# Cross-attention's keys and values projected in the first stage, y kept in SBUF

## The chip, the cores and the metric

The kernel runs on one core of a Trainium2 chip. The metric is the device time of one execution in microseconds, as the median of several runs. TensorE (PE in the profile) multiplies matrices, VectorE (DVE) and ScalarE (ACT) work elementwise, GpSimd (POOL) does a little beside them, and SyncE (SP) issues nearly all transfers. SBUF is the memory beside the engines, PSUM (`bank`, eight banks of 128 x 512 f32) takes TensorE's results, HBM holds inputs, output and scratch.

## The reference

One decoder layer over 8 batches of 512 tokens, width 512, in three sublayers, each with a norm. The first is a self-attention with 16 heads and fake quantisation: every tensor is divided by a power of two that comes from its own absolute maximum, rounded, and multiplied again. The second is a cross-attention to a context of 8 x 512 x 384, the third a feed-forward net. What matters here:

```python
h = layernorm(x) * fq_round(gamma) + fq_round(beta)
qkv = fq_floor(fq_floor(h) @ fq_round(w_qkv))
...
y = fq_floor(fq_floor(out) @ fq_round(w_out))
x1 = layernorm(x + y)
# cross-attention, 16 heads of 32
q = x1 @ Wq + bq
k = ctx_768 @ Wk + bk
v = ctx_768 @ Wv + bv
```

Keys and values of the cross-attention depend on the context alone; its queries depend on all of the self-attention.

## The kernel before

It is written by hand in stages. At the end of a stage every engine drains and calls `barrier(e, k)`, a semaphore that counts all five. The order of an engine's work is the order of the code; between engines semaphores alone set it (`wait_ge`, `then_inc`). SBUF is one `arena` that `Carve` divides anew for each stage, so a stage hands its results on through scratch in HBM. Batches run in loops of two (`batches`, `through`, `ahead`), with double buffers chosen by `par`.

**Start.** SP loads gamma, beta and the temperature (L409 to L411). VectorE takes the peaks of gamma and beta, GpSimd reduces them over the partitions (`over_partitions`), VectorE forms the powers of two (`power_of_two`) and the temperature's exponential. Then barrier 1, and only after it the first load of `x`.

**First norm** (`first_norm`, `turn_z`, `store_h`). For each batch VectorE takes statistics (`norm_stats`), writes the normed z (L1423), waits until TensorE has transposed its 16 tiles into PSUM (L788), applies gamma and beta from PSUM (L1437), and takes the peak of |h| (L1335 with `stats`). h goes to scratch, since its scale is known only after all batches. ScalarE issues the loads of `w_qkv` and `w_out` and computes nothing. After the last batch VectorE takes the peaks of the two weight matrices and quantises them (L1450 to L1453). Barrier 2; the next stage starts with the load of h (L437).

**Stages 3 to 7** size and compute the self-attention. Stage 7 leaves its result `oG` in SBUF.

**Stage 8**, the output projection (`project`, `y_out`, `quantise_o`, `peak_y`): TensorE projects, ScalarE copies PSUM into `yH`, VectorE takes the peak, SP stores `y` to scratch (`store_y`).

**Stage 9**, the cross-attention projections, per batch. SP loads context, x and y (L541 to L543). TensorE transposes the context (12 transposes, L931), computes V (12 matmuls, L938) and K (12, L943), transposes x1 (16, L950) and computes the queries (16, L957); each f32 matmul appears as two instructions in the trace. PSUM banks are claimed in turn. ScalarE evacuates every unit (`project_evac`: L1235 context, L1239 V, L1241 x1, L1245 K and queries with bias). VectorE quantises y, adds it to x and norms (L1634 on; `split_qk`), adds the value bias (L1642), and splits keys and queries into two f16 halves, which the next stage multiplies (L1647, L1648). SP stores x1, V and the halves; barrier 9 waits for them.

## Time and profile before

| what | value |
|---|---|
| median of 3 runs | 3355.82 us (3354.48 to 3357.97) |
| the profiled execution | 3351.47 us, its span 3349.7 us |
| TensorE busy | 2680.5 us, 80% of the span |
| VectorE busy | 2548.2 us, 76% |
| ScalarE busy | 1450.3 us, 43% |
| GpSimd busy | 158.8 us, 5% |
| moved between SBUF and HBM | 341 MB, mean 102 GB/s |
| mean granted clock of TensorE | 0.881 of full speed |

The span runs from the first to the last instruction on the chip. The shares are means over stages with different limits, so they say little of one stage. Times in the rows count from the span's start, and what ended an engine's idle time stands in brackets behind a row. DMA rows (SPq, ACTq) show the issue of transfers, not their duration. A granted clock of 1.00 is 2.4 GHz, 0.50 is 1.2 GHz.

### The profile page before, as it was taken

What the parts mean: (1) busy time and instruction counts of PE and PEld (TensorE: products, weight loads), DVE (VectorE), ACT (ScalarE), POOL (GpSimd) and SP (SyncE); (2) the same over time, 40 slices, a digit from 0 to 9 for tenths busy, and PEclk for the clock granted to TensorE, in tenths of its full rate; (3) what the DMA queues carried; (4) which work ended last, traced back from release to release, by engine and by line L of the source; (5) the groups of instructions that cost most, each with busy time, mean ns of one, the idle gap of its engine ahead of it and who ended that gap; (6) DMA issues with size and microseconds to landing.
All of it is one profiled execution on the core that took longest, in us unless ns stands there. A gap on an engine that the chain in (4) does not pass through costs nothing. (4 is left out here: it accounts for less than half of the span.)

```text
span 3349.7 us, 46340 instructions
## 1 busy us (share of the span) xinstructions
PE 2680.5 (80%) x13160; PEld 1043.6 (31%) x13160; DVE 2548.2 (76%) x4627; ACT 1450.3 (43%) x2397; POOL 158.8 (5%) x146
## 2 busy tenths in 40 slices
PE   1169899867777466667799979999999739999998
PEld 1124322211111233333344422222223324444443
DVE  5878599999999799998455559888886884544454
ACT  0000244359999899995222225555552002122111
POOL 0000233200000000000000000111110000000000
PEclk7579999955555799999899989999999959999999
DMA  5221122233333233332545543344445410100000
GB/s 201 100 82 63 63 88 108 99 104 126 120 123 113 98 109 94 104 97 73 191 169 175 175 119 90 102 111 111 108 152 204 180 42 1 49 27 26 25 26 26
DMA packets 198800, 341.15 MB, mean 102 GB/s; under 512 B 32536, under 2 KB 118552, under 8 KB 187280
## 3 DMA queue, kind: packets, MB, share of 16 engines
q1 hardware_dynamic: 194464, 322.90, 29.5%
q10 hardware_dynamic: 4208, 16.78, 1.3%
q8 instruction: 51, 0.84, 0.1%
q14 instruction: 77, 0.63, 0.1%
HBM read 200.70 MB, written 138.90 MB: 101 GB/s over the span
## 5 line engine op out<-in xcount | busy, mean ns | idle before, releaser
L1335 DVE TENSOR_REDUCE stats<-bank 128x1024 f32 (+1 forms) x352 | 408.0, 1217 | 66.3 <-PE bank L798 33.0
L1193 ACT ACTIVATE arena<-arena,scale 128x512 bf16<-128x512 int8 x512 | 408.1, 798 | 53.4 <-DVE arena L1530 53.4
L858 PE MATMUL bank<-arena 64*128 64x512 bf16 x512 | 306.1, 604 | 105.1 <-DVE arena L1523 66.8
L1211 ACT ACTIVATE arena<-arena,scale 128x512 f32<-128x512 int8 x512 | 367.1, 802 | 12.8 <-DMA arena<-dq_scr 12.8
L1523 DVE CUSTOM_DVE_ANT_0 arena<-bank,arena,fac 128x512 int8<-128x512 f32 x512 | 349.5, 746 | 23.5 <-PE bank L858 11.4
L1662 DVE TENSOR_REDUCE arena<-bank 128x2 f32<-128x1024 f32 x256 | 312.5, 1223 | 54.5 <-PE bank L968 38.7
L1279 ACT ACTIVATE arena<-bank 128x1024 f32<-128x1024 f32 x256 | 248.0, 1022 | 187.8 <-PE bank L984 187.8
L1313 ACT ACTIVATE arena<-bank,arena,fac 128x512 f32<-128x512 f32 x128 | 99.5, 777 | 456.8 <-PE bank L1136 456.8
L798 PE MATMUL bank<-arena 128*128 128x512 bf16 x1024 | 246.6, 385 | 60.9 <-DVE arena L1465 52.5
L1012 PE MATMUL bank<-arena 128*32 128x512 f32 x2048 | 270.1, 604 | 0.0
L875 PE MATMUL bank<-identb,arena 128*128 128x128 bf16 x2048 | 138.9, 222 | 148.7 <-DVE arena L1572 148.7
L1863 DVE TENSOR_SCALAR arena<-arena 128x512 f16<-128x512 f32 x128 | 54.7, 427 | 260.6 <-ACT arena L1313 260.6
L1144 PE MATMUL bank<-arena 128*128 128x512 f16 x1024 | 242.0, 379 | 1.7 <-DVE arena L1864 1.3
L1133 PE MATMUL bank<-arena 128*128 128x512 f16 x1024 | 241.9, 379 | 0.0
L1572 DVE TENSOR_SCALAR arena<-arena 128x512 bf16<-128x512 f32 x512 | 221.8, 480 | 24.8 <-ACT arena L1211 24.4
L875 PEld LDWEIGHTS bank<-identb,arena 128*128 128x128 bf16 x2048 | 116.7, 99 | 210.1 <-DVE arena L1572 166.6
L1181 ACT ACTIVATE arena<-bank,floor_c,fac 128x1024 int8<-128x1024 f32 x96 | 115.5, 1204 | 150.1 <-PE bank L798 95.6
L968 PE MATMUL bank<-arena 128*128 128x512 f16 x512 | 157.2, 391 | 22.3 <-DMA arena<-half_scr 13.4
L1688 DVE TENSOR_SCALAR arena<-arena 128x1024 f32<-128x1024 f32 (+1 forms) x192 | 165.9, 864 | 7.8 <-ACT arena L1279 7.8
L1181 ACT ACT_TABLE_LOAD x4 | 5.1, 1283 | 382.7 <-PE bank L798 382.7
L858 PEld LDWEIGHTS bank<-arena 64*128 64x128 bf16 x512 | 51.5, 101 | 359.8 <-DVE arena L1523 349.5
L1555 DVE TENSOR_SCALAR arena<-bank 128x2048 bf16<-128x2048 bf16 x128 | 155.7, 1216 | 0.0
(193 smaller groups left out, 3641.0 us busy)
## 6 DMA issues: line engine op xcount, KB each, us to landing
dq_scr<-arena SPq DMA_DIRECT2D x128, 256.0 KB, 2.0
arena<-dq_scr SPq DMA_DIRECT2D x128, 256.0 KB, 2.6
arena<-half_scr SPq DMA_DIRECT2D x256, 128.0 KB, 2.8
qkv_scr<-arena SPq DMA_DIRECT2D x8, 3072.0 KB, 9.6
arena<-in_x SPq DMA_DIRECT2D x16, 1024.0 KB, 7.1
arena<-qkv_scr SPq DMA_DIRECT2D x128, 128.0 KB, 2.3
x_scr<-arena SPq DMA_DIRECT2D x16, 1024.0 KB, 3.9
half_scr<-arena SPq DMA_DIRECT2D x32, 512.0 KB, 3.8
```

The costliest lines, as they stand in the source:

```text
L798: last = mm(dst, wqkv_q[:, k, P * u:P * u + P], hq[:, k, :], start=k == 0, stop=k == KC - 1)
L858: return mm(dst, qE[r, h // 2, P * t:P * t + P], kE[r, h // 2, :], start=True, stop=True)
L875: last = nc.tensor.transpose(PT[s % 2][:, j, P * t:P * t + P], aG[:, s % 2, t, P * j:P * j + P], identb[:, :])
L1012: last = mm(bank[XD * g:XD * g + XD, 7 if k < 2 else 6, :], w, eT[:, par, g, c, :], start=c == 0, stop=c == NT - 1)
L1133: mm(dst, Wf[:, k, P * s:P * s + P], xx[:, par, k, :], start=k == 0 and n == 0, stop=False)
L1144: mm(bank[:, t, :], gg[:, f % 3, P * t:P * t + P], Wp[:, f, :], start=f == 0 and n == 0, stop=False)
L1193: last = A(e_dump[:, NT * (h % 2) + t, :], dq8[:, h % 4, t, :], ACT.Exp, bias=negm_b[:, par, c:c + 1], scale=scale[:, S_DOTS:S_DOTS + 1], ...
L1211: A(eG[:, s % 2, t, :], dqG[:, s % 4, t, :], ACT.Exp, bias=negm_g[:, par, c:c + 1], scale=scale[:, S_DOTS:S_DOTS + 1]).then_inc(S("eG_done ...
L1279: A(eT[:, r % 2, 2 * a:2 * a + 2, c, :], bank[:, 2 + 2 * a:4 + 2 * a, :], ACT.Exp, scale=XSCALE / HALF ** 2).then_inc(S("eX_done"), 1)
L1335: return V.tensor_reduce(dst, src, ax, ALU.max, apply_absolute_value=True)
L1523: V.tensor_tensor_reduce(dq8[:, s, t, :], bank[:, 4 * (h % 2) + t, :], floor_row, fac[:, C_DOTS:C_DOTS + 1], -3.0e38, ALU.add, ALU.max, ac ...
L1662: V.tensor_reduce(mxX[:, mp, hs, 2 * u:2 * u + 2], bank[:, at:at + 2, :], AX.X, ALU.max).then_inc(S("sX_red"), 1)
```

## The change

Keys and values are projected in the first stage; barrier 1 is left out; `y` stays in SBUF; the later stage projects the queries alone.

- **SP** issues the loads of `x`, the context, `Wv`, `Wk`, the key bias (`bk16`) and the value bias (`bv_s`) at once behind gamma, beta and the temperature. In the first stage it also stores V and the key halves. Their completion is waited for at barrier 3. `Wq`, the query bias and the first two tiles of x for the residual are loaded during stage 8.
- **TensorE** in the first stage: context and V of batch 0, z's transposes of batch 0, K of batch 0; from then on z, context with V, and K of each batch. z takes banks 0 to 3, the rest takes banks 4 to 7 in turn (`kv_bank`). In stage 9 it transposes x1 one batch ahead of the queries.
- **ScalarE** applies gamma and beta (`h_out`, which was VectorE's L1437), and evacuates context, V and K in the first stage. In stage 8 it copies `y` into the part of `oG` that has been read (`y_of`).
- **VectorE** norms in place (`zB` is gone), one batch ahead. Gamma and beta are made ready after norm 0 (`gamma_beta`). The value bias and the key split come into the first stage. The peaks of the weights come in batch 2, their scales in batch 3, quantising in batches 3 to 5. In stage 9 the residual norm runs two batches ahead of the split of the queries.
- Loops over batches in these stages are written out.
- `y_scr` is gone; `first_norm`, its counters and the numbers of the partition reductions are renumbered to match.

The core of the diff (removed lines are left out where new code stands in their place):

```diff
-            barrier(sp, 1)
...
+            load_x(0)
+            load_ctx(0)
+            for dst, src in ((Wv_s, Wv), (Wk_s, Wk)):
+                sp.dma_start(dst, chunk(src)).then_inc(S("wI_in"), 16)
+            load_x(1)
+            with nc.allow_non_contiguous_dma(reason="a column of 512 numbers"):
+                sp.dma_start(bk16, col(bk)).then_inc(S("wI_in"), 16)
+            sp.dma_start(bv_s, bv.rearrange("(a n) -> a n", a=1).broadcast_to([P, D])).then_inc(S("wI_in"), 16)
+            load_ctx(1)
...
+            for b in range(NB):
+                if b + 2 < NB:
+                    sp.wait_ge(S("z_turned"), b * NT + NT)
+                    load_x(b + 2)
+                    sp.wait_ge(S("kv_mm"), b * UNITS_K + CC)
+                    load_ctx(b + 2)
+                sp.wait_ge(S("h_ready"), b * KC + KC)
+                sp.dma_start(h_scr[b], hB[:, b % 2]).then_inc(S(f"h_stored{b % 2}"), 16)
+                sp.wait_ge(S("v_ready"), b * NT + NT)
+                for o in range(KC):
+                    sp.dma_start(v_scr[b * KC + o], vI[:, :, P * o:P * o + P]).then_inc(S("v_stored"), 16)
+                sp.wait_ge(S("split_done"), b * KC + KC)
+                for n in (0, 1):
+                    sp.dma_start(half_scr[2 + n][b * KC:b * KC + KC].rearrange("o p t -> p o t"), k_halves[:, n]
+                                 ).then_inc(S("k_stored"), 16)
...
+            def load_x1(b):
+                if b >= 2:
+                    sp.wait_ge(S(f"x_in{b % 2}"), 8 * NB + 16 * (b // 2))
+                sp.dma_start(x1_of[b % 4], tok(x[b])).then_inc(S(f"x_in{b % 2}"), 16)
+            sp.dma_start(Wq_s, chunk(Wq)).then_inc(S("wI_in"), 16)
+            with nc.allow_non_contiguous_dma(reason="a column of 512 numbers"):
+                sp.dma_start(bq16, col(bq)).then_inc(S("wI_in"), 16)
+            for b in (0, 1):
+                load_x1(b)
...
+            for b in (2, 3):
+                load_x1(b)
+            for b in range(NB):
                 sp.wait_ge(S("x1_ready"), b + 1)
...
+                sp.dma_start(x1_scr[b], x1_of[b % 4]).then_inc(S("x1_stored"), 16)
+                sp.wait_ge(S("split_done"), (NB + b) * KC + KC)
+                for n in (0, 1):
+                    sp.dma_start(half_scr[n][b * KC:b * KC + KC].rearrange("o p t -> p o t"), q_halves[:, b % 2, n]
+                                 ).then_inc(S(f"q_stored{b % 2}"), 16)
+                if b + 4 < NB:
+                    sp.wait_ge(S("x1_turned"), b * KC + KC)
+                    sp.wait_ge(S("x1_stored"), 16 * b + 16)
+                    load_x1(b + 4)
...
+            pe.wait_ge(const_made, 7)
...
+            def kv_bank(b, n):
+                before = b * UNITS_K + n - 4 if n >= 4 else (b - 1) * UNITS_K + (UNITS_K - 3 + n if n < 3 else UNITS_K - 4)
+                if before >= 0:
+                    pe.wait_ge(S("kv_evac"), before + 1)
+                return bank[:, 4 + n % 4, :]
+            def ctx_values(b):
+                pe.wait_ge(S(f"c_in{b % 2}"), 16 * (b // 2) + 16)
+                for k in range(CC):
+                    dst = kv_bank(b, k)
+                    for t in range(NT):
+                        last = nc.tensor.transpose(dst[:, P * t:P * t + P], cx[:, b % 2, t, P * k:P * k + P], ident[:, :])
+                    last.then_inc(S("kv_mm"), 1)
+                for t in range(NT):
+                    dst = kv_bank(b, CC + t)
                     if t == 0:
...
+                        pe.wait_ge(S("kv_evac"), b * UNITS_K + CC)
+                    for k in range(CC):
+                        last = mm(dst, cxT[:, k, P * t:P * t + P], Wv_s[:, k, :], start=k == 0, stop=k == CC - 1)
+                    last.then_inc(S("kv_mm"), 1)
+            def ctx_keys(b):
+                for o in range(KC):
+                    dst = kv_bank(b, CC + NT + o)
+                    for k in range(CC):
+                        last = mm(dst, Wk_s[:, k, P * o:P * o + P], cxT[:, k, :], start=k == 0, stop=k == CC - 1)
+                    last.then_inc(S("kv_mm"), 1)
+            pe.wait_ge(S("wI_in"), 16 * 4)
+            ctx_values(0)
+            turn_z(0)
+            ctx_keys(0)
+            for b in range(1, NB):
+                turn_z(b)
+                ctx_values(b)
+                ctx_keys(b)
...
+            def queries(b):
+                pe.wait_ge(S("x1T_done"), b * KC + KC)
                 for o in range(KC):
...
+                    if b:
+                        pe.wait_ge(S("q_evac"), (b - 1) * KC + o + 1)
                     for k in range(KC):
...
+                        last = mm(bank[:, 4 + o, :], Wq_s[:, k, P * o:P * o + P], x1T[:, b % 2, k, :],
+                                  start=k == 0, stop=k == KC - 1)
+                    last.then_inc(S("q_mm"), 1)
+            turn_x1(0)
+            for b in range(NB):
+                if b + 1 < NB:
+                    turn_x1(b + 1)
+                queries(b)
...
+            def h_out(b):
+                act.wait_ge(S("z_turned"), b * NT + NT)
+                if b >= 2:
+                    act.wait_ge(S(f"h_stored{b % 2}"), 16 * (b // 2))
+                    act.wait_ge(S("h_peak"), b - 1)
+                for k in range(KC):
+                    A(hB[:, b % 2, k, :], bank[:, k, :], ACT.Identity, bias=bet[:, k:k + 1], scale=gam[:, k:k + 1]
+                      ).then_inc(S("h_ready"), 1)
+            def values_kept(b):
+                for n in range(CC + NT):
+                    act.wait_ge(S("kv_mm"), b * UNITS_K + n + 1)
+                    src = bank[:, 4 + n % 4, :]
+                    if n < CC:
+                        A(cxT[:, n, :], src, ACT.Copy).then_inc(S("kv_evac"), 1)
+                    else:
+                        if n == CC and b:
+                            act.wait_ge(S("v_stored"), 64 * b)
+                        A(vI[:, n - CC, :], src, ACT.Copy).then_inc(S("kv_evac"), 1)
+            def keys_kept(b):
+                for o in range(KC):
+                    n = CC + NT + o
+                    act.wait_ge(S("kv_mm"), b * UNITS_K + n + 1)
+                    if b:
+                        act.wait_ge(S("split_done"), (b - 1) * KC + o + 1)
+                    A(t32[:, o, :], bank[:, 4 + n % 4, :], ACT.Identity, bias=bk16[:, o:o + 1], scale=HALF
+                      ).then_inc(S("kv_evac"), 1)
+            values_kept(0)
+            act.wait_ge(S("gam_ready"), 1)
+            act.wait_ge(S("b16_ready"), 1)
+            h_out(0)
+            keys_kept(0)
+            for b in range(1, NB):
+                h_out(b)
+                values_kept(b)
+                keys_kept(b)
...
+            def x1_turned_out(b):
+                for k in range(KC):
+                    act.wait_ge(S("x1_turned"), b * KC + k + 1)
+                    if k == 0 and b >= 2:
+                        act.wait_ge(S("q_mm"), (b - 1) * KC)
+                    A(x1T[:, b % 2, k, :], bank[:, k, :], ACT.Copy).then_inc(S("x1T_done"), 1)
+            def queries_out(b):
+                for o in range(KC):
+                    act.wait_ge(S("q_mm"), b * KC + o + 1)
+                    if b:
+                        act.wait_ge(S("split_done"), (NB + b - 1) * KC + o + 1)
+                    A(q32[:, o, :], bank[:, 4 + o, :], ACT.Identity, bias=bq16[:, o:o + 1], scale=HALF
+                      ).then_inc(S("q_evac"), 1)
+            x1_turned_out(0)
+            for b in range(NB):
+                if b + 1 < NB:
+                    x1_turned_out(b + 1)
+                queries_out(b)
...
+            def h_peak(b):
+                dve.wait_ge(S("h_ready"), b * KC + KC)
+                amax(stats[:, b:b + 1], hB[:, b % 2], AX.XY).then_inc(S("h_peak"), 1)
...
+            first_norm(0)
+            gamma_beta()
+            for b in range(NB):
+                h_peak(b)
+                if b + 1 < NB:
+                    first_norm(b + 1)
+                bias_values(b)
+                if b == 2:
+                    weight_peaks()
+                if b == 3:
+                    weight_scales()
+                if b in (3, 4):
+                    quantise_wqkv(2 * b - 6)
+                    quantise_wqkv(2 * b - 5)
+                if b == 5:
+                    quantise_wout()
+                split_keys(b)
...
+            def residual_norm(b):
+                ch = Chain(dve, S("norm_step"), 2 + NORM, b, NB * NORM)
+                x1 = x1_of[b % 4]
+                dve.wait_ge(S(f"x_in{b % 2}"), 8 * NB + 16 * (b // 2) + 16)
+                ch.link(V.tensor_scalar(y8, y_of[b], fac[:, C_Y:C_Y + 1], FLOOR, ALU.mult, ALU.add))
+                ch.link(V.scalar_tensor_tensor(x1, y8, sc(S_Y), x1, ALU.mult, ALU.add))
+                norm_stats(ch, x1)
                 for t in range(NT):
...
+                    last = normed(x1[:, t, :], x1[:, t, :], t)
                 last.then_inc(S("x1_ready"), 1)
...
+            for b in (0, 1):
+                residual_norm(b)
+            for b in range(NB):
+                if b + 2 < NB:
+                    residual_norm(b + 2)
+                split_queries(b)
```

## Rows read from the trace of the kernel before

**Rows 1.** Windows of two stages; columns: us, busy time (instructions) by engine, PEclk, DMA share, GB/s.
```profile
23.00:149.00 126.00, 28.91 (x128) 26.06 (x128) 95.15 (x234) 0.00 (x0) 0.00 (x0) 0.61 0.53 196
1620.00:1964.00 344.00, 308.74 (x864) 147.61 (x864) 173.39 (x369) 90.73 (x152) 0.00 (x0) 0.96 0.50 173
```

**Rows 2.** Timeline of the first stage; columns: start, duration, engine, line, operation.
```profile
23.37 1.15 SPq L419 DMA_DIRECT2D arena<-in_x  x2
...
31.85 2.13 ACTq L1171 DMA_DIRECT2D arena<-in_L_attn_w_qkv  x4
...
43.91 2.46 DVE L1398 BATCH_NORM_STATS2 bn<-arena 128x6 f32<-128x512 f32 x4
...
53.70 2.96 DVE L1437 TENSOR_SCALAR arena<-bank,gam,bet 128x512 f32<-128x512 f32 x4 [2.47 <-PE bank L788]
...
56.78 2.29 DVE L1335 TENSOR_REDUCE stats<-arena 128x2048 f32 x1
...
58.98 2.46 DVE L1398 BATCH_NORM_STATS2 bn<-arena 128x6 f32<-128x512 f32 x4
```

**Rows 3.** Timeline of the weight work after the first norm.
```profile
149.59 17.41 DVE L1335 TENSOR_REDUCE peak<-arena 128x1 f32<-128x12288 f32 x2
...
169.27 1.82 DVE L1450 TENSOR_SCALAR arena<-arena,inv 128x3072 int8<-128x3072 f32 x1
...
188.83 1.06 SPq L437 DMA_DIRECT2D arena<-h_scr  x2
```

**Rows 4.** Timeline of one batch of the cross-attention projections.
```profile
1677.56 1.68 PE L931 MATMUL bank<-ident,arena 128*128 128x128 f32 x12
...
1690.58 2.49 DVE L1642 TENSOR_TENSOR arena<-arena 128x512 f32<-128x512 f32 x4
...
1700.74 1.91 PE L950 MATMUL bank<-ident,arena 128*128 128x128 f32 x16
...
1701.02 0.69 ACT L1245 ACTIVATE arena<-bank,arena 128x512 f32<-128x512 f32 x1 [1.89 <-PE bank L943]
...
1701.61 2.05 ACT L1241 ACTIVATE arena<-bank 128x512 f32<-128x512 f32 x4
...
1702.20 0.69 DVE L1648 TENSOR_TENSOR arena<-arena 128x512 f16<-128x512 f32 x1
...
1703.71 14.00 PE L957 MATMUL bank<-arena 128*128 128x512 f32 x32 [1.06 <-ACT arena L1241]
...
1717.55 1.68 PE L931 MATMUL bank<-ident,arena 128*128 128x128 f32 x12
```

**Rows 5.** Groups of instructions on the page: the GELU evacuation.
```profile
L1313 ACT ACTIVATE arena<-bank,arena,fac 128x512 f32<-128x512 f32 x128 | 99.5, 777 | 456.8 <-PE bank L1136 456.8
```

**Rows 6.** Timeline at both ends of the cross-attention stage.
```profile
1619.35 0.16 DVE L1624 TENSOR_TENSOR fac<-fac,inv 128x1 f32<-128x1 f32 x1
...
1620.82 0.40 SPq L529 DMA_DIRECT2D arena<-in_L_xattn_Wq  x1
...
1632.02 0.17 DVE L1629 TENSOR_SCALAR arena<-arena 128x8 f32<-128x8 f32 x1 [12.50 <-DMA arena<-in_L_xattn_bv]
...
1639.25 1.29 DVE L1634 TENSOR_SCALAR arena<-arena,fac 128x2048 int8<-128x2048 f32 x1 [7.07 <-DMA arena<-y_scr]
...
1650.20 2.49 DVE L1642 TENSOR_TENSOR arena<-arena 128x512 f32<-128x512 f32 x4
...
1958.97 0.69 DVE L1648 TENSOR_TENSOR arena<-arena 128x512 f16<-128x512 f32 x1
```

**Rows 7.** Windows around idle stretches of TensorE and its restart.
```profile
0.00:41.00 41.00, 3.48 (x16) 3.24 (x16) 15.34 (x64) 0.00 (x0) 1.88 (x12) 1.00 0.35 127
1614.00:1618.00 4.00, 0.00 (x0) 0.00 (x0) 2.92 (x5) 0.33 (x1) 0.36 (x1) 1.00 0.11 45
1958.00:1961.00 3.00, 0.00 (x0) 0.00 (x0) 1.12 (x2) 0.47 (x1) 0.00 (x0) 0.83 0.11 38
1634.00:1642.00 8.00, 7.18 (x17) 4.27 (x18) 2.71 (x2) 1.79 (x3) 0.00 (x0) 0.50 1.04 394
```

More of the change, by code:

```diff
@@ L40 @@
 DUOS = QKV_UNITS // 2
[L41 removed]
+UNITS_K = CC + NT + KC
 NEXT_AT = (7, 9, 11, 13)
@@ L905, in project @@
                 for t in range(NT):
-                    pe.wait_ge(S("y_evac"), b * NT + t + 1)
+                    if not (isinstance(b, int) and b < 2):
+                        pe.wait_ge(S("y_evac"), b * NT + t + 1 - 2 * NT)
                     for k in range(PAIRS):
@@ new lines, in split_keys @@
+            def split_keys(b):
+                ch = Chain(dve, S("split_step"), KC, b)
+                if b:
+                    dve.wait_ge(S("k_stored"), 32 * b)
+                for o in range(KC):
+                    dve.wait_ge(S("kv_evac"), b * UNITS_K + CC + NT + o + 1)
+                    ch.link(V.tensor_copy(k_halves[:, 0, o, :], t32[:, o, :]))
+                    V.tensor_tensor(k_halves[:, 1, o, :], t32[:, o, :], k_halves[:, 0, o, :], ALU.subtract
+                                    ).then_inc(S("split_done"), 1)
+                ch.end()
@@ new lines, in _ @@
+            first_norm(0)
+            gamma_beta()
+            for b in range(NB):
+                h_peak(b)
[12 more added lines that the diff above has]
+                split_keys(b)
@@ L1615, in quantise_o @@
                     peak_y(b - 1, 1 - par)
-            through(dve, quantise_o)
+            for b in range(NB):
+                quantise_o(b, b % 2)
             peak_y(NB - 1, 1)
-            dve.wait_ge(S("y_peak"), 2 + NB)
+            dve.wait_ge(S("y_peak"), NB)
             link(amax(peak[:, S_Y:S_Y + 1], stats[:, 0:NB]))
@@ L1650, in split_qk, with split_queries @@
-                ch.end()
-            batches(dve, split_qk)
+                ch.end()
+            def split_queries(b):
+                ch = Chain(dve, S("split_step"), KC, b, NB * KC)
+                if b >= 2:
+                    dve.wait_ge(S(f"q_stored{b % 2}"), 32 * (b // 2))
+                for o in range(KC):
+                    dve.wait_ge(S("q_evac"), b * KC + o + 1)
+                    ch.link(V.tensor_copy(q_halves[:, b % 2, 0, o, :], q32[:, o, :]))
+                    V.tensor_tensor(q_halves[:, b % 2, 1, o, :], q32[:, o, :], q_halves[:, b % 2, 0, o, :], ALU.subtract
+                                    ).then_inc(S("split_done"), 1)
+                ch.end()
@@ L1652, in _ @@
+            for b in (0, 1):
+                residual_norm(b)
+            for b in range(NB):
+                if b + 2 < NB:
+                    residual_norm(b + 2)
+                split_queries(b)
             barrier(dve, 9)
```

330 lines of the change are left out of this document (113 added, 217 removed).

## The prediction

> **What bounds the kernel now.** I began with windows cut at the barriers, which show how busy each engine is by stage, and went to timelines of one batch in the two stages that the change touches, to see which wait ends last. The others (369 to 1548 us, and from 1964) keep their instructions, and I give them no change.
>
> The windows show two opposite stages [rows 1]. From 23 to 149 us TensorE is busy 28.9 of 126 us, VectorE 95.2, and ScalarE not at all. From 1620 to 1964 TensorE is busy 309 of 344 us, VectorE half, ScalarE a quarter. In the first stage a batch takes 15.07 us, from one row of statistics (43.91) to the next (58.98), and the chain is VectorE's own: norm, wait for TensorE's transposes (2.47), gamma and beta (2.96), peak [rows 2]. After the eighth batch VectorE alone runs 39 us, the weight peaks of 17.4 us and the quantising; the next stage's first load goes out at 188.83 [rows 3]. In the cross-attention stage a batch takes 39.99 us (1677.56 to 1717.55), and TensorE waits in it about 2 us in all, 1.06 of it ahead of the queries [rows 4]. VectorE there waits for ScalarE, which waits for TensorE: the stage is TensorE's.
>
> So TensorE's work is carried from a stage that it fills to one where it has room. What it costs there depends on what the first stage becomes.
>
> **The first stage after.** Each batch gives TensorE 16 transposes of z (1.91 us, as 1700.74), 12 of the context (1.68, as 1677.56), and 24 instructions for V and 24 for K. The 32 for the queries take 13.84 us (1703.71 to 1717.55), 0.4325 each, so V and K take 20.8 [rows 4]. ScalarE evacuates in program order: four h tiles, then three context tiles, then V, then K; V cannot start before the third context tile is out. Counted from the end of z's transposes that is 0.28 us to ScalarE's start (K ends at 1700.74, the copy starts at 1701.02), four h tiles, three copies and 0.1 to hand over. Plain copies run at a pitch of 0.51 us (four in 2.05) [rows 4]. An evacuation with a per-partition scale and bias appears only as the GELU, 777 ns [rows 5]. The one with a bias alone takes 0.69 us (1701.02) and is the nearest; overlapped a little I take 0.67 a tile, with 0.51 and 0.78 as ends. The gap is 0.28 + 2.7 + 1.56 + 0.1 = 4.65 us, of which the context's transposes fill 1.7: TensorE stands idle for 2.9. The period is 1.91 + 4.65 + 20.8 = **27.3 us** (26.7 to 27.8).
>
> VectorE must fit under it. Norm and peak take 15.07 - 2.96 - 2.47 = 9.6 us [rows 2], the norm alone 7.3; gamma and beta go to ScalarE. The value bias takes 2.5, the key split 4 x 1.15 = 4.6 (0.43 + 0.69 and the step between them) [rows 4]: 16.7, so 10.6 are spare. In batches 2 to 5 VectorE also has the peaks (17.4), the scales (1.6) and quantising (169.27 to 188.6, 19.3) [rows 3]: 38.3 against 42 spare. They stand ahead of the key split. From the end of z's transposes: batch 2's value bias ends at 16.6, the peaks at 34.0, its split at 38.6, that is 11.3 into batch 3; then peak and norm 4 end at 20.9, and TensorE wants norm 4 at 25.4. These 4.5 us are the tightest place; batch 3 ends about 10 into batch 4, batch 4 about 7 into batch 5, and batch 5 catches up. ScalarE waits for the split of the batch before only from 18 us on. I cost the weight work at nothing, under TensorE's V and K; without that cover it costs up to its 38 us.
>
> The start: the first load moves from 23.37 to about 2.3 us. TensorE waits for both matrices and both biases, which stand behind x0, context 0 and x1 on SP's queue, 4.7 MB. Before the value bias freed VectorE (1632.02), 2.9 MB took 11.2 us from 1620.82 [rows 6]; with 2 us of latency the same rate gives 17 us, so 19 on the clock (16 to 23). ScalarE first waits for x1 and issues five weight loads (four in 2.13 us, [rows 2]), so V of batch 0 starts near 23 and ends at 33.4, z's transposes at 35.3, K at 45.7. Seven periods lead to 236.8. Last evacuation and split take 2.15 (1700.74 to the end of the subtraction, 1702.89, [rows 4]), scale and barrier 2.4 (from 167.0, where the peaks end, to 169.27, [rows 3], and a product). Two key stores stand ahead of the first h load, 1 us. **The load goes out at 242.4 in place of 188.8: +53.6.**
>
> **The clock.** TensorE's granted clock is 1.00 (2.4 GHz) over the first 41 us, so I count its first work there at full speed. It fell inside the 3 us after the queries (1958 to 1961, mean 0.83), but stayed up through 4 us idle from 1614, and in the cross-attention stage it stayed at 0.50 through the first 8 us of work [rows 7]. An idle stretch of 2.9 us in each batch lies inside that scatter. A fall costs half of the time at the low clock, up to 4 us. I take three falls in seven batches at 2.3: **+7**, with 0 and 7 x 3 = 21 as bounds. The Trainium skill (TensorE: Matmul & The Clock Gate, "HAM oscillation — how this bites in real kernels") describes a loop whose wait between bursts drops the clock in every iteration. By that the sum takes the upper bound, 3243 us; the trace bears it out halfway, with a fall in one idle stretch of this length and none in a longer one.
>
> **Stage 8.** Matmuls, evacuations and peaks stay. `y` no longer goes out and comes back; that was hidden, but for the last store: VectorE is done at 1619.51, SP's next issue comes at 1620.82 [rows 6]. The loads of `Wq` and of x0 and x1 now run beside the output projection.
>
> **The query stage.** VectorE starts at about 1619.9. A residual norm takes 11.0 us (1639.25 to 1650.20, [rows 6]), and TensorE's order puts the transposes of batch 1 ahead of batch 0's queries, so it waits for two norms: 1641.9. Then 16 transposes at the low clock (28.91 us / 128 x 16 = 3.6, [rows 1]) and the queries with 1.2 us until the clock rises: 1660.6. A period is 1.91 + 13.84 = 15.75 us on TensorE; the 1.06 goes, since x1's tiles are copied a batch ahead. On VectorE it is 11.0 + 4.6 = 15.6. VectorE works ahead: norm b+3 ends 13.1 us after the queries of b, where 15.7 are allowed. Seven periods lead to 1770.9, the last split to **1773.0**; now it ends at 1958.97 + 0.69 = 1959.66 [rows 6]: **-186.6**. The last stores before the next barrier stay.
>
> **Sum**: +53.6 + 7 - 186.6 = -126 us. The profiled execution took 3351.5 us (span 3349.7); that gives 3225.5, a ratio of 0.9624. The three runs have a median of 3355.8, and by the ratio **3229 us**. They lie within 0.1%; 0.2%, 7 us, is about what can be told from no change.
>
> **Rivals.**
> - *The clock falls in every batch of the first stage.* For it: the fall at 1958 to 1961. Against: 4 us without one. It adds 14: 3243.
> - *VectorE sets one of the new stages.* Only 0.15 us separate the engines in the query stage, 4.5 us cover the weight work. Each us over in the query period costs 7: with 1 to 2, 3236 to 3243. Against: operations and shapes are the known ones.
> - *TensorE stays at the low clock (1.2 GHz) through the first stage.* This one could end slower. For it: the stage has a mean of 0.61 now [rows 1]. Transposes then take 3.6 in place of 1.9, matmuls 0.865 in place of 0.4325: 22.5 us a batch, 180 in all less the 7 counted: 3402, 1.4% slower. It decides from 133 / 22.5, the sixth of eight batches, on. Against: the same instructions ran at full speed later on (0.96 over that stage), with gaps near 1 us.
> - *No fall, earlier loads, evacuation at the lower bound*: 3229 - 7 - 3 - 4 = 3215.
>
> **Chances.** Forecast 0.66 (its own range 3217 to 3240), clock in every batch 0.12, VectorE 0.11, early and undisturbed 0.07, low clock throughout 0.03, something else 0.01. The range 3212 to 3252 leaves out the last two and the tails of the others. Only the low clock throughout and part of the rest is not faster: 0.96, 0.01, 0.03.
>
> **What would show it.** After: a first-stage period near 27.3 us with TensorE idle 2.9 us until ScalarE's copy of the context; clock mostly 1.00; peaks in batch 2 and no wait of TensorE for a norm; first h load near 242; a query period of 15.75 us, its first queries behind two norms. The forecast fails if V starts much later than 4.65 us after z's transposes, if whole batches run at 0.50, if TensorE waits for VectorE among the queries, or if its first instruction comes after 23 us.

## The result and the profile after

The changed kernel takes 3226.9 us (median of four runs, 3225.4 to 3229.4), the kernel before 3355.2 in the same measurement: a ratio of 0.9617, with a 95% interval of 0.9601 to 0.9634. The forecast was 3229 us, a ratio of 0.9624. Its profiled execution took 3229.4 us (span 3227.4) against 3351.5 (span 3349.7).

The timeline of TensorE in the first stage of the changed kernel (start, duration, engine, line, operation, count; in brackets the idle time ahead and who ended it; L787 are z's transposes, L802 the context's, L809 V, L816 K):

```profile
18.45 2.79 PE L802 MATMUL bank<-ident,arena 128*128 128x128 f32 x12 [18.45 <-DMA arena<-in_L_xattn_bv]
22.98 13.59 PE L809 MATMUL bank<-arena 128*128 128x512 f32 x24 [1.74 <-ACT arena L1203]
...
49.56 1.94 PE L787 MATMUL bank<-ident,arena 128*128 128x128 f32 x16 [0.94 <-DVE arena L1469]
...
55.92 12.23 PE L809 MATMUL bank<-arena 128*128 128x512 f32 x24 [3.12 <-ACT arena L1203]
...
84.63 13.47 PE L809 MATMUL bank<-arena 128*128 128x512 f32 x24 [3.11 <-ACT arena L1203]
...
136.87 1.91 PE L787 MATMUL bank<-ident,arena 128*128 128x128 f32 x16
138.61 1.47 PE L802 MATMUL bank<-ident,arena 128*128 128x128 f32 x12
143.20 10.54 PE L809 MATMUL bank<-arena 128*128 128x512 f32 x24 [3.12 <-ACT arena L1203]
153.58 10.46 PE L816 MATMUL bank<-arena 128*128 128x512 f32 x24
163.88 1.91 PE L787 MATMUL bank<-ident,arena 128*128 128x128 f32 x16
```

Read it for three things. The order of a batch is as forecast, and one that runs undisturbed takes 163.88 - 136.87 = 27.01 us. In front of V of batches 1 to 7 TensorE waits 3.12 us for ScalarE's last context copy, which stands behind the four h tiles (ScalarE's rows of the same batch, L1195 the h tiles, L1203 the context copies):

```profile
138.81 2.78 ACT L1195 ACTIVATE arena<-bank,bet,gam 128x512 f32<-128x512 f32 x4 [1.06 <-PE bank L787]
141.48 1.58 ACT L1203 ACTIVATE arena<-bank 128x512 f32<-128x512 f32 x3
```

And the same 24 instructions of V take 10.54 us in two of these seven batches and 12.2 to 13.5 in the other five. There the clock had fallen, as the windows over the start of V in batch 2 (slow) and over V in batch 4 (not slow) show, with a granted clock of 0.50 and 1.00 (the columns are those of [rows 1]):

```profile
84.63:90.50 5.87, 5.87 (x7) 2.50 (x8) 5.31 (x21) 0.37 (x1) 0.00 (x0) 0.50 0.98 314
143.20:153.70 10.50, 10.50 (x25) 4.76 (x26) 9.84 (x27) 1.79 (x3) 0.00 (x0) 1.00 0.60 187
```

The waits of TensorE from 45 to 252 us (total, times, longest) say that nothing else holds it up; VectorE's weight work, which stands at 99.37 us now and not behind the last batch [rows 3], doesn't appear:

```profile
PE bank L809 <- ACT arena L1203: 21.8, 7, 3.1
PE bank L787 <- DVE arena L1469: 0.9, 1, 0.9
```

```profile
99.37 17.40 DVE L1387 TENSOR_REDUCE peak<-arena 128x1 f32<-128x12288 f32 x2
...
253.98 1.11 SPq L452 DMA_DIRECT2D arena<-h_scr  x2
```

The last of these rows is SP's first load of the next stage, 253.98 where it was 188.83 [rows 3]: +65.2 us. The windows (columns as in [rows 1]) show how full TensorE's new stage is, 178 of 200 us, and the query stage, 129 of 154 us:

```profile
50.00:250.00 200.00, 177.84 (x530) 88.59 (x528) 147.39 (x267) 65.27 (x105) 0.53 (x1) 0.94 0.49 162
1684.00:1838.00 154.00, 128.59 (x384) 65.80 (x384) 117.00 (x275) 38.45 (x64) 0.00 (x0) 0.90 0.45 150
```

The query stage on TensorE (L959 the transposes of x1, L968 the queries):

```profile
1695.62 3.64 PE L959 MATMUL bank<-ident,arena 128*128 128x128 f32 x16 [17.30 <-DVE arena L1469]
1706.47 3.67 PE L959 MATMUL bank<-ident,arena 128*128 128x128 f32 x16 [7.21 <-DVE arena L1469]
1709.94 14.85 PE L968 MATMUL bank<-arena 128*128 128x512 f32 x32
1724.63 1.91 PE L959 MATMUL bank<-ident,arena 128*128 128x128 f32 x16
1726.38 13.90 PE L968 MATMUL bank<-arena 128*128 128x512 f32 x32
1740.12 1.91 PE L959 MATMUL bank<-ident,arena 128*128 128x128 f32 x16
```

TensorE waits for two norms, as forecast, and never after: 15.48 us a batch (1740.12 - 1724.63). The stage lasts 149.2 us, from 1684.14 (the scale factors are done) to 1833.33 (the last subtraction, 1832.64 + 0.69); before it lasted 340.15, from 1619.51 to 1959.66 [rows 6]: -191.0.

So the profile adds up: +65.2 for the first stage, -0.5 for everything between (1430.7 us before, 1430.2 after), -191.0, and +4.0 behind the query stage's last subtraction. That is -122.3, the difference of the spans.

### The profile page after: what moved, and what is told of

It is laid out like the page before. It is cut to its first block and busy times, and to the rows that moved or that the text cites. A ratio compares the mean times of both kernels' runs of the same rounds, so it can differ in the third digit from the quotient of the medians.

```text
span 3227.4 us, 45086 instructions
## 1 busy us (share of the span) xinstructions
PE 2676.8 (83%) x13112; PEld 1038.7 (32%) x13160; DVE 2525.0 (78%) x4604; ACT 1469.1 (46%) x2426; POOL 156.2 (5%) x147
## 5 line engine op out<-in xcount | busy, mean ns | idle before, releaser
L832 PE MATMUL bank<-arena 128*128 128x512 bf16 x989 | 242.4, 385 | 23.5 <-DVE arena L1560 13.5
L1160 PE MATMUL bank<-arena 128*128 128x512 f16 x1024 | 242.0, 379 | 1.2 <-DVE arena L1967 0.8
L1149 PE MATMUL bank<-arena 128*128 128x512 f16 x1024 | 241.9, 379 | 0.0
L984 PE MATMUL bank<-arena 128*128 128x512 f16 x512 | 157.6, 391 | 22.6 <-DMA arena<-half_scr 13.4
L992 PE MATMUL bank<-arena 128*128 128x512 f16 x512 | 155.4, 387 | 0.5 <-ACT arena L1331 0.2
```

The source lines that it names most:

```text
L832: last = mm(dst, wqkv_q[:, k, P * u:P * u + P], hq[:, k, :], start=k == 0, stop=k == KC - 1)
L1149: mm(dst, Wf[:, k, P * s:P * s + P], xx[:, par, k, :], start=k == 0 and n == 0, stop=False)
L1160: mm(bank[:, t, :], gg[:, f % 3, P * t:P * t + P], Wp[:, f, :], start=f == 0 and n == 0, stop=False)
```

## The experiments

Each was timed in turn with the kernel before on one chip. A difference to the changed kernel is (its ratio - 0.9617) x 3355 us. A ratio is known to 0.0013 to 0.0016, so such a difference is known to some 7 us; what is smaller than that I read from the trace.

### The clock, and the idle time in front of V

Twelve more transposes in the gap; their result is overwritten unused.

```diff
+                if b:
+                    dst = kv_bank(b, CC)
+                    for n in range(12):
+                        nc.tensor.transpose(dst[:, P * (n % 4):P * (n % 4) + P], Wv_s[:, n % CC, 0:P], ident[:, :])
                 for t in range(NT):
                     dst = kv_bank(b, CC + t)
```

> The changed kernel with 12 more transposes in each batch from the second on, between the context's transposes and V, into the bank that V overwrites next; their result is not used. They fill 2.7 us (12 of 0.23 us) of the 3.12 us in which TensorE waits for ScalarE's copies. Theory (the 3.12 us of idle in front of V are what makes the granted clock fall): V takes 10.5 us in every batch from the second on, in place of 12.2 to 13.5 in five of seven, and the run ends 8 to 11 us earlier than the changed kernel, at 3216 to 3219 us. Rival 1 (the clock falls for another reason, so many busy and idle phases together or the time of the run): V keeps its 12 to 13.5 us in most batches and the time is 3225 to 3228. Rival 2 (added work only adds): 3 us of idle are replaced, up to 0.5 us a batch late, so up to 3230.

Measured: 3219.2 us, ratio 0.9586 (0.9573 to 0.9599), -10 us. TensorE's timeline, a batch that was slow in the changed kernel (L807 are the added ones, L813 is V):

```profile
77.87 1.47 PE L802 MATMUL bank<-ident,arena 128*128 128x128 f32 x12
79.18 1.47 PE L807 MATMUL bank<-ident,arena 128*128 128x128 f32 x12
82.46 10.54 PE L813 MATMUL bank<-arena 128*128 128x512 f32 x24 [1.81 <-ACT arena L1207]
```

All seven V take 10.54 us, and the window from 50 to 240 us has a clock of 1.00. The added work did not even fill the gap: 12 more transposes take 1.31 us at full clock (79.18 - 77.87), not the 2.7 I had used, which is their price at the low one, and 1.81 us of idle remain. Cutting the idle from 3.12 to 1.81 us was enough. Every batch still takes 27.01 us, so the whole gain is the clock's. In the changed kernel the falls cost 10.8 us (the V times over 10.54, summed).

Then the order that removes the gap itself:

```diff
-                turn_z(b)
-                ctx_values(b)
+                ctx_turn(b)
+                turn_z(b)
+                ctx_values(b)
...
-                h_out(b)
-                values_kept(b)
+                values_kept(b, range(CC))
+                h_out(b)
+                values_kept(b, range(CC, CC + NT))
```

> The changed kernel with the context's 12 transposes ahead of z's 16 in each batch from the second on, and ScalarE's three copies of the context tiles ahead of its four h tiles. Theory (the 3.12 us in front of V are there because ScalarE works off the four h tiles, 2.8 us, before it copies the context tiles): V follows z's transposes without idle, the period of a batch falls from 27.0 to 23.9 us, and with no idle in front of V the clock doesn't fall: 7 x 3.12 = 22 us and up to 11 us more, so 3194 to 3205 us, the stage's last split 22 to 33 us earlier. Rival 1 (VectorE then sets the period: its 38 us of weight work in batches 2 to 5 have only 4.5 us of slack against a period of 27.3): TensorE waits for the norms in batches 4 to 6, and 8 to 15 of the 22 us are lost: 3212 to 3220. Rival 2 (the idle time moves to K's copies or the next z transposes): within 3 us of 3227.

Measured: 3194.8 us, ratio 0.9518 (0.9505 to 0.9531), -33 us, all that the theory gave it. TensorE's timeline (L811 is V, L818 K):

```profile
119.14 1.60 PE L802 MATMUL bank<-ident,arena 128*128 128x128 f32 x12
120.58 1.91 PE L787 MATMUL bank<-ident,arena 128*128 128x128 f32 x16
122.33 10.47 PE L811 MATMUL bank<-arena 128*128 128x512 f32 x24
132.63 10.46 PE L818 MATMUL bank<-arena 128*128 128x512 f32 x24
142.93 1.59 PE L802 MATMUL bank<-ident,arena 128*128 128x128 f32 x12
144.82 1.94 PE L787 MATMUL bank<-ident,arena 128*128 128x128 f32 x16 [0.29 <-DVE arena L1474]
```

Nothing stands in front of V, and a batch takes 23.79 us (142.93 - 119.14). The bracket in the last row is TensorE's only wait in batches 1 to 7, 0.29 us for VectorE at batch 5: the weight work still fits, with nothing left over.

### The h tiles back on VectorE

```diff
             def h_peak(b):
-                dve.wait_ge(S("h_ready"), b * KC + KC)
+                dve.wait_ge(S("z_turned"), b * NT + NT)
+                if b >= 2:
+                    dve.wait_ge(S(f"h_stored{b % 2}"), 16 * (b // 2))
+                for k in range(KC):
+                    V.tensor_scalar(hB[:, b % 2, k, :], bank[:, k, :], gam[:, k:k + 1], bet[:, k:k + 1],
+                                    ALU.mult, ALU.add).then_inc(S("h_ready"), 1)
+                dve.wait_ge(S("h_ready"), b * KC + KC)
```

> The changed kernel with the four h tiles of a batch computed on VectorE, as the kernel before did, in place of ScalarE. VectorE has 147 us of work in the 200 us of the loop; the h tiles add 8 x 2.8 = 22. Theory (ScalarE's h tiles stand in front of its context copies and make 1.3 of the 3.1 us in front of V; VectorE has the slack for them): the idle time in front of V falls to about 1.9 us as in the filled variant, the clock doesn't fall, and the time is 3208 to 3214 us, 15 to 20 below the changed kernel. Rival 1 (VectorE becomes the bound, as the prediction's second rival had it): TensorE waits for norms in batches 4 to 6 and the time is 3226 to 3243. Rival 2 (the idle time gets shorter, but the clock falls as before): 3217 to 3222.

Measured: 3204.7 us, ratio 0.9549 (0.9536 to 0.9562), -23 us: more than expected, since only 0.88 us of idle remain in front of V, not 1.9. TensorE's timeline shows both sides of the trade, the row of V (L809) and the worst of three waits for a norm (L787):

```profile
149.98 2.42 PE L787 MATMUL bank<-ident,arena 128*128 128x128 f32 x16 [3.05 <-DVE arena L1458]
152.20 2.70 PE L802 MATMUL bank<-ident,arena 128*128 128x128 f32 x12
155.67 10.54 PE L809 MATMUL bank<-arena 128*128 128x512 f32 x24 [0.78 <-ACT arena L1195]
```

VectorE, at 163 of 176 us, costs 0.75 + 3.05 us in batches 4 and 5, as the first rival had it in kind. It is small beside the 2.24 us x 7 of idle and the falls of the clock that go. Here the clock dips during the transposes behind the 3.05 us (2.70 us for those that take 1.47 elsewhere) and is back before V.

### The weight work behind the last batch again

```diff
-                if b == 2:
-                    weight_peaks()
...
                 split_keys(b)
+            weight_peaks()
+            weight_scales()
+            for k in range(KC):
+                quantise_wqkv(k)
+            quantise_wout()
```

> The changed kernel with the peaks, the scales and the quantising of the two weights moved back behind the eighth batch. Theory (the prediction costed this work at nothing while TensorE sets the period of a batch): 38 us of VectorE's work come back behind the last split, less the 1 or 2 us that the smaller stall elsewhere gives, so 3262 to 3267 us; the period of a batch without a clock fall stays 27.0 us. Rival 1 (in the loop the work delayed norms or splits, so that TensorE paid part of it already): the loop of eight batches gets shorter by more than 3 us, and the run ends under 3260. Rival 2 (the work could hide under the tail of stores behind the last batch in any case): under 10 us later.

Measured: 3266.8 us, ratio 0.973 (0.9715 to 0.9745), +38 us. On VectorE's timeline the work stands alone, from its first row to the row that follows it:

```profile
246.09 17.40 DVE L1387 TENSOR_REDUCE peak<-arena 128x1 f32<-128x12288 f32 x2
...
284.98 0.16 DVE L1387 TENSOR_REDUCE peak<-stats 128x1 f32<-128x8 f32 x1
```

That is 38.9 us, as costed, and an undisturbed batch takes 27.01 us without the work in the loop too. The execution in this trace is the shortest of four (3258.7 us, the others 3266.7 to 3267.0), and its last K ends 5.4 us earlier than in the changed kernel (244.26 against 249.65), which looks like the first rival. But all of it is the clock: the falls in front of V cost 6.1 us here and 10.8 there, and V(0) takes 12.85 us and not 13.59. So both rivals fall: inside the loop the weight work cost TensorE nothing.

### The first barrier

```diff
-STAGES = (2, 3, 5, 6, 7, 8, 9, 10, 11, 12, 13)
+STAGES = (1, 2, 3, 5, 6, 7, 8, 9, 10, 11, 12, 13)
...
+            barrier(sp, 1)
```

(and the same line on the other four engines, VectorE's behind the scaling of gamma and beta).

> The changed kernel with the first barrier put back: the loads of x, the context and the weights start only when gamma, beta and the temperature are done on VectorE. Theory (leaving the barrier out moved every load forward): in the changed kernel the first load goes out at 2.3 us and V(0) starts at 23.0; in the kernel before the first load of x went out at about 23 us. TensorE's first transposes need x, the context and all the first loads, some 16 us after they go out, so V(0) starts at about 42 to 44 us and the run ends 18 to 21 us later than the changed kernel's: 3245 to 3248 us. Rival (the start was bound by something else, the norm's chain on VectorE for instance): under 8 us later, at most 3235.

Measured: 3241.9 us, ratio 0.966 (0.9645 to 0.9675), +14 us: the direction of the theory, short of its 18 to 21. TensorE's timeline:

```profile
34.94 2.79 PE L805 MATMUL bank<-ident,arena 128*128 128x128 f32 x12 [34.94 <-DMA arena<-in_L_xattn_bv]
39.57 10.57 PE L812 MATMUL bank<-arena 128*128 128x512 f32 x24 [1.84 <-ACT arena L1207]
```

The first load of x goes out at 19.14 us and not at 23.37 [rows 2], because the new code computes the temperature while GpSimd reduces the peaks of gamma and beta, not behind it; so 4 us of the earlier start are owed to this reordering. The theory had counted them to the barrier. TensorE starts 16.5 us later than without the barrier, and V(0) then runs at full clock, 10.57 us against 13.59. The two together are +13.5 us.

### The query stage: y kept, the early loads, the order of the transposes

The shorter batch makes most of the 191 us: 39.99 us before [rows 4] and 15.48 now are 7 x 24.51 = 171.6 us. The first two experiments price parts of the rest, the third an order that the change could have had.

y stored and loaded again, into the same place:

```diff
+            for b in range(NB):
+                sp.wait_ge(S("y_peak"), b + 1)
+                sp.dma_start(y_scr[b], y_of[b]).then_inc(S("v_stored"), 16)
+            sp.wait_ge(S("v_stored"), 64 * NB + 16 * NB)
             barrier(sp, 8)
+            for b in (0, 1):
+                load_y(b)
```

> The changed kernel with y stored to HBM in the stage that computes it and loaded again, into the same place in SBUF, in the stage of the queries; all else as in the changed kernel. Theory (the load of y(0) stands in front of the first residual, the other loads are hidden under 15.5 us batches): the stage of the queries starts 3 to 5 us later, and the stage before it ends up to 2 us later for its last store: 3230 to 3236 us. Rival 1 (all is hidden): 3225 to 3229. Rival 2 (the traffic disturbs more than the start: 16 loads of 1 MB and 8 stores each delay batches): over 3240.

Measured: 3233.7 us, ratio 0.9631 (0.9617 to 0.9646), +5 us, which the ratios alone can't tell from none. VectorE's timeline has it at the place named, the first residual behind a wait for SP at the barrier (its last store) and one for the load:

```profile
1683.10 0.17 DVE L1737 TENSOR_SCALAR arena<-arena 128x4 f32<-128x4 f32 x1 [1.50 <-SPq L222]
1687.97 1.29 DVE L1743 TENSOR_SCALAR arena<-arena,fac 128x2048 int8<-128x2048 f32 x1 [4.69 <-DMA arena<-y_scr]
```

The other seven loads are hidden: a batch still takes 15.48 us.

The stage's first loads behind the barrier:

```diff
-            sp.dma_start(Wq_s, chunk(Wq)).then_inc(S("wI_in"), 16)
...
             barrier(sp, 8)
 
+            sp.dma_start(Wq_s, chunk(Wq)).then_inc(S("wI_in"), 16)
```

(with `bq` and the first two `load_x1`).

> The changed kernel with the loads of Wq, bq and of the first two x of the queries' stage issued behind the eighth barrier and not ahead of it. Theory (the part of the gain that comes from the early loads): in the changed kernel the first residual starts 0.4 us after the barrier; with these loads behind it, it waits for bq and x(0), which land 6 and about 10 us after their issue, so the stage starts 9 to 11 us later: 3236 to 3240 us. Rival (VectorE or TensorE catch it up, since VectorE's norms run ahead of TensorE): under 4 us later.

Measured: 3237.5 us, ratio 0.9651 (0.9636 to 0.9667), +11 us. VectorE's timeline:

```profile
1686.63 0.17 DVE L1725 TENSOR_SCALAR arena<-arena 128x4 f32<-128x4 f32 x1 [6.51 <-DMA arena<-in_L_xattn_bq]
1689.65 1.29 DVE L1731 TENSOR_SCALAR arena<-arena,fac 128x2048 int8<-128x2048 f32 x1 [2.85 <-DMA arena<-in_x]
```

9.4 us of waits where the changed kernel has 0.2. So 9 of the 191 us come from this and not from the work that left the stage.

The x1 transposes in the middle of the queries:

```diff
-                if b + 1 < NB:
-                    turn_x1(b + 1)
-                queries(b)
+                queries(b, (0, 1))
+                if b + 1 < NB:
+                    turn_x1(b + 1)
+                queries(b, (2, 3))
```

> The changed kernel with the next batch's x1 transposes put in the middle of a batch's queries: two tiles of Q(b), then the turn of batch b+1, then the other two tiles; ScalarE's copies in the same order. Theory (TensorE waits 7.2 us for the second norm although it could already work on Q(0), and is busy without a gap after that): the first two tiles of Q(0) run in the time of the second norm, TensorE's whole work starts 10.9 - 3.7 = 7.2 us earlier, and the stage's last split comes 6 to 8 us earlier: 3219 to 3222 us. Rival (VectorE sets this stage: 15.6 us a batch against TensorE's 15.5, and its norms aren't any earlier): Q waits for splits and norms, and 0 to 2 us are gained: 3225 to 3228 us.

Measured: 3221.8 us, ratio 0.9596 (0.9583 to 0.9609), -7 us. TensorE's timeline:

```profile
1696.25 3.64 PE L959 MATMUL bank<-ident,arena 128*128 128x128 f32 x16 [17.29 <-DVE arena L1471]
1700.58 9.49 PE L968 MATMUL bank<-arena 128*128 128x512 f32 x16 [0.69 <-ACT arena L1287]
1709.90 1.91 PE L959 MATMUL bank<-ident,arena 128*128 128x128 f32 x16
```

The 7.21 us wait of TensorE for the second norm is gone, the first two tiles of Q(0) run in it, and the stage is 6.8 us shorter (142.1 in place of 148.9, from its first residual). VectorE does not set it.

### Both orders, and an earlier start

First the context's transposes ahead of z's and the x1 transposes among the queries in one kernel, by the edits shown above:

> Both orders at once: the context's transposes ahead of z's in the first stage, and the x1 transposes in the middle of the queries. Theory (the two stages share nothing, so that the gains add): 32 to 35 us of the first and 6 to 8 of the second below the changed kernel, 3185 to 3191 us. Rival (the second order gains nothing, VectorE sets the stage): 3193 to 3197 us.

Measured: 3186.2 us, ratio 0.949 (0.9477 to 0.9503), -43 us. The gains add.

What was left in the first stage was the start, where TensorE waits for `bv` until 18.5 us. The next two kernels load context(0) and `Wv` first and let TensorE wait for no more than it needs:

```diff
-            load_x(0)
             load_ctx(0)
-            for dst, src in ((Wv_s, Wv), (Wk_s, Wk)):
-                sp.dma_start(dst, chunk(src)).then_inc(S("wI_in"), 16)
+            sp.dma_start(Wv_s, chunk(Wv)).then_inc(S("c_in0"), 16)
+            load_x(0)
+            sp.dma_start(Wk_s, chunk(Wk)).then_inc(S("wI_in"), 16)
...
-            pe.wait_ge(S("wI_in"), 16 * 4)
+            ctx_turn(0)
             ctx_values(0)
             turn_z(0)
+            pe.wait_ge(S("wI_in"), 16 * 4)
```

> Both orders, and an earlier start: context(0) and Wv are loaded first, TensorE waits for these two alone before its first transposes and for Wk and the bias rows only before K(0); ScalarE issues the loads of the quantised weights behind its first copies; VectorE takes norm 1 ahead of the peak of h(0). Theory (TensorE's start at 18.5 us is set by the last bias row, bv, and by the loads that ScalarE waits to issue, not by what V(0) needs): context(0) and Wv land at 11 to 13 us, V(0) starts at 16 to 18 us in place of 23.1, K(0) and batch 1 follow without a stall, and the time falls by 5 to 7 us against the kernel with both orders: 3179 to 3182 us. Rival 1 (norm 0 or norm 1 is then late: x(0) lands later, and VectorE needs 8 us for each norm): 0 to 2 us are gained, 3184 to 3187. Rival 2 (the clock: V(0) starts right after a shorter wait and runs at the low level for longer): half of it is lost, 3182 to 3184.

Measured: 3192.9 us, ratio 0.9516 (0.9503 to 0.953): 9 us slower by the ratio than both orders alone. The theory and both rivals were wrong. TensorE's timeline, and ScalarE's row that ends the wait:

```profile
14.35 13.46 PE L812 MATMUL bank<-arena 128*128 128x512 f32 x24 [0.69 <-ACT arena L1204]
...
63.96 12.55 PE L819 MATMUL bank<-arena 128*128 128x512 f32 x24 [10.62 <-ACT arena L1208]
```

```profile
63.31 2.06 ACT L1208 ACTIVATE arena<-bank 128x512 f32<-128x512 f32 x4 [17.45 <-DMA v_scr<-arena]
```

V(0) began 8.7 us earlier, and then batch 1's K (L819) stood behind a V evacuation (L1208) for 10.6 us. ScalarE's evacuation waits until the values of the batch before are in HBM, and these four stores took 20.1 us (median) from issue to landing (8.4 MB of weights had gone out at 27.9 us on ScalarE's queue, just ahead of them). To test that, the five loads move ahead of ScalarE's first copies of V, and their wait for x goes:

```diff
-            values_kept(0)
-            for par in (0, 1):
-                act.wait_ge(S(f"x_in{par}"), 16)
+            values_kept(0, range(CC))
             for k in range(KC):
                 act.dma_start(wqkv_f[:, k, :], chunk(w_qkv)[:, k, :]).then_inc(S("wA_in"), 16)
             act.dma_start(wout_f, chunk(w_out)).then_inc(S("wA_in"), 16)
+            values_kept(0, range(CC, CC + NT))
```

> The early start with ScalarE's five loads of the quantised weights (8 MB) issued at about 14 us, right behind its three copies of the context tiles, in place of 27.9 us. In the early start V(0) began at 14.4 us, 8.7 earlier than with both orders, but the store of V(0) took 20 us to land behind these loads and TensorE stood still for 10.6 us in batch 1. Theory (that collision is all that ate the gain): issued 14 us sooner, the loads are through before the first V tiles are stored at about 30 us, as they are in the kernel with both orders, the 10.6 us and the 2.1 us of the low clock behind them go, and the time is 8 us under the kernel with both orders: 3177 to 3181 us. Rival (they now collide with x(1), Wk and the bias rows, so that K(0) or norm 1 waits): half or more of it is lost, 3182 to 3188.

Measured: 3178.7 us, ratio 0.9473 (0.946 to 0.9486), the fastest of all: 48 us under the changed kernel, 5.3% under the kernel before. Against both orders alone the ratios give 6 us, which they can't tell from none; in the traces the last K ends 9.0 us earlier (206.57 against 215.58). All waits of TensorE up to 220 us:

```profile
PE bank L803 <- POOL floor_c L724: 10.8, 1, 10.8
PE bank L812 <- ACT arena L1204: 0.7, 1, 0.7
PE bank L788 <- DVE arena L1476: 0.3, 1, 0.3
```

The stall is gone, but not quite for the reason expected, that the loads would be through before the first V tiles are stored. The last of them was issued at 15.61 and landed 32.0 us later, and the first four stores still took 14.5 us (median) to land. ScalarE waited for them:

```profile
52.19 2.06 ACT L1208 ACTIVATE arena<-bank 128x512 f32<-128x512 f32 x4 [6.80 <-DMA v_scr<-arena]
```

The wait ends at 52.19, and TensorE finishes V of the same batch at 52.87 (42.40 + 10.47) and goes on without idle time. So the collision is shorter now and ends just in time. TensorE's start hangs on GpSimd's masks at 10.8 us and no longer on a load.

### The kernel before, once more

> The kernel before, profiled once more. In the two profiles read so far the part behind the queries' stage took 1385.3 us before and 1389.4 after, with the same code. Theory (a spread between executions): its 29 groups from the first division on GpSimd to the reduction of the last weights' peaks take 666 to 672 us, as in the five profiles with the new code. Rival (the new placement of the tiles makes this stage slower): 665 to 666.5 us again, below all five of the new code (667.8 to 672.1).

Measured in the quantity expected: 669.1 us, so the rival falls. The whole part behind the ninth barrier, whose code is the same everywhere, took 1385.3 and 1388.4 us in two profiles of the kernel before, and between 1386.0 and 1392.4 in the twelve profiles of the changed kernel and its variants. The +4.0 us of the sum is inside that spread.

## Why the prediction was right

By its own steps, against the profile of the changed kernel:

- **The start.** TensorE's first instruction at 18.45 (19 forecast), V(0) at 22.98 (23). In front of ScalarE's first copy stands a table load of 1.28 us that the forecast did not have. The first barrier was worth 14 us.
- **V(0).** Forecast at full clock, 10.4 us, since a granted clock of 1.00 was shown over the first 41 us [rows 7]. It took 13.59, and K(0) ended 2.9 us late. This step failed, by a misread row: [rows 7] has 16 transposes in 3.48 us in that window, where 16 take 1.91 at full clock [rows 4]. So the column said 1.00 while TensorE ran at half pace. It does so again here. The first 7 instructions of V(0) take 6.02 us under a column of 1.00, as long as the 7 under 0.50 in batch 2 (the first window of this kind above):

```profile
22.98:29.00 6.02, 6.02 (x7) 2.50 (x8) 0.00 (x0) 0.49 (x1) 0.00 (x0) 1.00 1.02 433
```

  At the start of these traces the pace has to be read from the durations. Why V(0) takes 10.57 us in some executions and up to 13.6 in others stays open. The start is not always slow: with the barrier back, V(0) took 10.57, and in the variant with the h tiles on VectorE 10.57 from the same 23.0 us.
- **The period.** 27.01 us against 27.3: 3.12 us of idle against 2.9, four h tiles in 2.78 us against 2.7. From z's first transpose to V it is 6.33 us (6.56 forecast), for V and K 20.68 (20.8). -2.0 us in seven.
- **The clock.** "Three falls in seven batches at 2.3", +7, was right in kind and near in size, with the wait for ScalarE as the cause, which the filled gap and the other order show. Six profiles that keep this gap have 3 to 5 falls in seven and lose 6.1 to 10.8 us; the one shown has 5 and 10.8. The number three was chosen between the bounds 0 and 7, not derived. The falls come in a regular order, which the forecast did not have (see the end). The Trainium skill (TensorE: Matmul & The Clock Gate, "HAM oscillation — how this bites in real kernels") has the mechanism, a wait between bursts that drops the clock; that it does so in every iteration, the rival of 3243, these traces don't bear out.
- **The weight work at nothing.** Right, and the term that mattered most: 38 us with the cover gone. The slack was real as well: norm 4 ends at 130.77 and its transposes start at 136.87, 6.1 us where 4.5 were forecast. With a period of 23.79 a wait of 0.29 is left.
- **The end of the stage.** First load 253.98 against 249.4, 4.6 us late: +2.9 (V(0)), +0.9 (norm 1, not forecast), +3.8 (falls, 10.8 for 7), -2.0 (periods), -1.2 (the end after the last K, 4.3 us in place of 5.55), 4.4 in sum.
- **The query stage.** -191.0 against -186.6. Two norms first, then TensorE alone, as forecast. The 4.4 us are 7 x 0.27 = 1.9 in the period (the durations of rows that follow on each other overlap by 0.17 us, which I had added up), and 1.7 for a slip in counting: behind Q(0) stand seven batches of queries but only six of transposes, since those of batch 1 come ahead of Q(0). The rest, 0.8, is in the stage's two ends.
- **Stage 8, and the rest.** No change, within the spread between executions.

The two errors in the first stage and in the query stage, +4.6 and -4.4, cancel. The sum for the profiled execution, -126, is then 3.7 us from the measured -122.3, nearly all of it the +4.0 behind the query stage. And the profiled execution is the longest of the four, 2.5 us over the median. So most of the exactness of 3229 against 3227 is luck, while its direction and size are not. Of the rivals, VectorE setting a stage is ruled out for the changed kernel by its waits; it shows itself at a period of some 24 us.

## What to carry to other kernels

Work moved from a full engine into a stage where it has room costs what its new chain costs, not what its instructions do. Here the period of the first stage rose from 15.07 to 27.01 us, 12 us for some 22 us of TensorE's work. 3 of the 27 us were an evacuation queue in the wrong order, and the idle time costs a second time through the clock. Look for the copy that ends such a wait and put it ahead of what nobody waits for yet. And when a start is pulled forward, follow the large transfers that stay behind: they meet the first stores in a place where nothing waited before.

## What the runs showed that I had not expected

- Idle stretches of TensorE of 3.12 us before the same work are followed by a fall of the clock in some batches and not in others (V of 10.54, 12.2 and 13.5 us in one profile). They come in a regular order: in batches 1 to 7 of all six profiles with this gap a V of 13.4 to 13.5 us is followed by one of 12.1 to 12.2, then by two of 10.54, then by 13.5 again (V(1) alone can stand outside it, 12.23 ahead of 13.47 in the changed kernel). Where this order begins differs, and with it the number of falls. After stretches of 1.81 and 0.88 us no V behind the first batch was slow.
- V of batch 0, behind 18 us without work, 12 transposes and a wait of about 2 us, took 10.57 us in one, 12.2 to 12.9 in five and 13.5 to 13.6 in three of the profiles of the changed kernel and eight variants with the same start, and 10.57 behind 35 us without work.
- Stores of 256 KB that take 3.1 us to land in the variant with both orders took 20.1 us behind 8.4 MB of loads from the other queue, and 14.5 with the loads issued 14 us sooner. In the early start with the late loads, the load of x(2), issued at 29.6, landed late as well, and VectorE waited 2.12 us for it.
